# A two-layer graph attention network on one core: more sorted blocks, merged query products, a third fill bank, and exponentials kept beside the messages

## The chip, the core and the metric

The kernel runs on one core of a Trainium2 chip. The metric is the time of one execution on the device in microseconds; lower is better. The core has five engines that run their own instruction streams and meet at semaphores: PE (matrix products), DVE (vector work), ACT (activations and copies), POOL (here: indirect DMAs) and SP (plain DMAs).

## The reference

6250 nodes with 128 features and 200,000 edges, sorted by destination, with random sources. Each node also has an edge to itself. Two layers, 8 heads of 16:

```
loops = arange(n); src = [src, loops]; dst = [dst, loops]
for l in range(2):
    xn  = layernorm(x) * ln1_g + ln1_b
    deg = out-degree of each node, standardised
    xp  = xn + xn @ Wpos + bpos + deg * Wdeg + bdeg
    q, k, v = xp @ Wq + bq, xp @ Wk + bk, xp @ Wv + bv        # [n, 8, 16]
    att = clip(sum(q[dst] * k[src], -1) / 4, -50, 50)
    ex  = exp(att - segment_max(att, dst))
    aggr = segment_sum(v[src] * ex / segment_sum(ex, dst)[dst], dst)
    x = x + aggr @ Wo + bo
    x = x + gelu(layernorm(x) @ W1 + b1) @ W2 + b2
out = layernorm(input x + x)
```

## The kernel before

**Tables.** For each layer a table of keys and values (kv_table, 1 KB a node) and one of queries (q_table) lie in HBM. A prelude of about 280 us computes the first ones, the degrees and plans of the edges. The last steps of each node of layer 1 write its rows of layer 2's tables, and layer 2 starts when all are written.

**Two kinds of units.** The 49 tiles of 128 destination nodes are worked off in two ways.
- Most go by *chunks* of 1024 edges (8 tiles of 128 edges). `gather` (L1971, POOL) fetches the key and value rows of a chunk with 8 indirect DMAs, whose indices lie in SBUF (src_idx); four chunk buffers (kv_ring, and kv_last in the arena) take turns, and a buffer is free when the chunk's messages are made.
- The last NBS[l] tiles (8 in layer 1, 10 in layer 2) are *sorted blocks*: the edges of a tile are sorted by their source's tile during the run (`sort_vector`, `sort_tensor`), at most 128 to each pair of tiles. A tile is then 7 blocks (OB) of 7 edge tiles (TB). Their source rows come by one plain DMA into source_rows and are spread to the edges on PE by products with one-hot matrices (`source_by_edge` L940, `gather_rows` L952), and copied to kv_block by ACT (`copy_rows` L1238).

Layer 1 has 165 chunks and 56 blocks, layer 2 157 and 70. `unit_order` spreads the blocks among the chunks from chunk FIRST_B on.

**One unit.** PE computes distances between an edge's place and each node into one of two PSUM banks (*fills*, `fill_bank`; L962 "turn", L970 "hot"), ACT turns them into one-hots (L1227). PE spreads queries to the edges (L993 for a chunk, L1026 for a block) into two PSUM banks, DVE multiplies them by the keys in two operations (L1676), reduces to scores (L1685), clips (L1688, L1691); ACT takes the exponential twice, into PSUM (ex, L1260) and beside the messages in SBUF (msg, L1263); DVE multiplies the values by ex (L1700, the messages); PE sums them by destination (L1009, L1042), and DVE adds the sum to a ring of windows of 64 nodes (L1726) or to the block's row (L1731).

**The order** is written out: each engine's stream is a loop over slots, two a unit. In slot 2u PE makes the fills for unit u+2 and spreads unit u+1, DVE makes scores of u and products of u+1, ACT the exponentials of u; in slot 2u+1 DVE makes the messages of u and adds the sums of u-1, PE sums u-1. The 33 (27) steps of finished nodes and the steps of the sorts hang on the slots behind that. `exact_scale` (L1377) is the last part of a layernorm's scale, one short chain of three DVE steps, 196 times; L1896 and L1901 add degree and bias to a node's new q, k, v.

Of the kernel before, what the change touches and what calls it, by code (L numbers as in the profile page):

```python
# [68 lines left out]
OUT_TILES = 6  # L69
NEWTON = 3  # L70
# [5 lines left out]
NBS = 8, 10  # L76
# [13 lines left out]
RING_W = 32  # L90
AHEAD = 8
# [15 lines left out]
class Layer:  # L107


    def __init__(self, l, before):  # L110
# [10 lines left out]
        assert all(b - a > 2 for a, b in zip(self.block_at, self.block_at[1:]))  # L121
# [169 lines left out]
def graph_transformer(nc, x, src, dst, Wq, bq, Wk, bk, Wv, bv, Wo, bo, Wpos, bpos, Wdeg, bdeg,  # L291
                      ln1_g, ln1_b, ln2_g, ln2_b, W1, b1, W2, b2, out):
    with ExitStack() as ctx:
# [49 lines left out]
        small = sb("small", [P, 1])  # L343
# [24 lines left out]
        kv_block = part_of(TB * 2 * D).rearrange("p (t d) -> p t d", t=TB)  # L368
# [90 lines left out]
        tile_firsts = early[0:NS, free + 2 * SEG + 3 * P:free + 2 * SEG + 3 * P + SEG // P]  # L459
        block_firsts, tiles_before = (early[0:NS, o:o + NB] for o in range(free + 2 * SEG + 3 * P + SEG // P, free + 2 * SEG + 3 * P + SEG // P + 2 * NB, NB))  # L460
        o_less = free + 2 * SEG + 3 * P + SEG // P + 2 * NB
# [10 lines left out]
        ex = psum[:, 3, 0:T * H].rearrange("p (t h) -> p t h", t=T)  # L472
        apart = [psum[:, 4 + i, :] for i in range(2)]
# [16 lines left out]
        def edge_sum(l, u):  # L490
# [56 lines left out]
        next_ready, deg_row, qkv_ready, x_added = (  # L547
            semaphore(n) for n in ("next_ready", "deg_row", "qkv_ready", "x_added"))
# [11 lines left out]
        def bank_free(e, m, held):  # L560
# [4 lines left out]
            if before >= 0:  # L565
# [3 lines left out]
                elif name == "totals":  # L569
                    e.wait_ge(sort_total, (SA + 1) * j + 1)  # L570
                elif name.startswith("slots"):
                    e.wait_ge(sort_read, (SA + 3) * j + int(name[5:]) + 1)
                elif name.startswith("rank"):
                    e.wait_ge(sort_picked, 3 * (SA * j + int(name[4:])) + 1)
                else:
                    e.wait_ge(bank_read[name], nth(l, j, name))
# [348 lines left out]
        def fill_bank(e, k):  # L925
            if k >= 2:
                e.wait_ge(apart_read, k - 1)
            return apart[k % 2]

        def one_hots_made(e, k, since):  # L930

            if since < k + 2:
# [141 lines left out]
        def node_tensor(e, l, j, k, held):  # L1074
# [147 lines left out]
        def one_hots(e, to, n, what, h):  # L1222
# [4 lines left out]
            e.activation(to[:, at:at + width], apart[k % 2][:, 0:width], ACT.Relu, bias=1.0, scale=-1.0  # L1227
                         ).then_inc(apart_read, 1)

        def copy_rows(e, n, i):  # L1230

            m = part_of_unit(n)
            if m >= 1 and i == 0:
                e.wait_ge(msg_ready, block_unit(m - 1) + 1)
# [3 lines left out]
            e.copy(kv_block[:, ts[0]:ts[-1] + 1, :].rearrange("p t d -> p (t d)"), apart[k % 2][:, 0:len(ts) * 2 * D]  # L1238
# [15 lines left out]
        def make_exp(e, l, u):  # L1254
# [28 lines left out]
        def node_scale(e, l, j, i):  # L1283
# [4 lines left out]
            e.activation(tiny[:, 8:9], tiny[:, 7:8], ACT.Ln, bias=small[:, 0:1]).then_inc(norm_log, 1)  # L1288
            e.wait_ge(norm_log, n)
# [370 lines left out]
        def make_products(e, l, u):  # L1660
            n = unit(l, u)
            what, i = LAYERS[l].units[u]
            for h in range(2):
                f = 2 * n + h
                ts = part_tiles(l, u, h)
                rows = slice(ts[0], ts[-1] + 1)
                e.wait_ge(spread, f + 1)
                if what == "chunk":
                    m = chunk(l, i)
                    if h == 0:  # L1670
                        e.wait_ge(gathered[m % RING_KV], 16 * T * (m // RING_KV + 1))
                    keys = kv[m % RING_KV][:, rows, 0:D]
                else:
                    e.wait_ge(apart_read, fill(n, "rows", 2 * h + 1) + 1)
                    keys = kv_block[:, rows, 0:D]
                e.tensor_tensor(prod[:, ts[0] * P:(ts[-1] + 1) * P].rearrange("p (t d) -> p t d", d=D),  # L1676
# [510 lines left out]
```

## Time and profile before

| | us |
|---|---|
| median of 3 runs (3645.29 to 3647.68) | 3647.36 |
| span of the profiled execution | 5559.9 |
| busy in it: PE / DVE / POOL / ACT | 3461.6 / 2916.7 / 2472.4 / 1771.1 |

The page tells the share of each engine, the granted clock of TensorE by slices, the chain that ended last and the costliest groups. A group's row is: line, engine, operation, out<-in with shapes, count | busy us in all, mean ns of one | idle time of the engine just before them, and what ended most of it. "issue" is idle time for which the profile shows no reason, "remote" a wait whose cause it doesn't show. A row of the timeline is: start, duration, engine, line and operation, in brackets the idle time before. The profiled execution is much longer than a timed one.

### The profile page before, as it was taken

What the parts mean: (1) busy time and instruction counts of PE and PEld (TensorE: products, weight loads), DVE (VectorE), ACT (ScalarE), POOL (GpSimd) and SP (SyncE); (2) the same over time, 40 slices, a digit from 0 to 9 for tenths busy, and PEclk for the clock granted to TensorE, in tenths of its full rate; (3) what the DMA queues carried; (4) which work ended last, traced back from release to release, by engine and by line L of the source; (5) the groups of instructions that cost most, each with busy time, mean ns of one, the idle gap of its engine ahead of it and who ended that gap; (6) DMA issues with size and microseconds to landing.
All of it is one profiled execution on the core that took longest, in us unless ns stands there. A gap on an engine that the chain in (4) does not pass through costs nothing.

```text
span 5559.9 us, 72300 instructions
## 1 busy us (share of the span) xinstructions
PE 3461.6 (62%) x24196; PEld 2666.6 (48%) x24475; DVE 2916.7 (52%) x6780; ACT 1771.1 (32%) x4391; POOL 2472.4 (44%) x2597
## 2 busy tenths in 40 slices
PE   5834656655665656666566376666666566666666
PEld 4623445444454445444444254455555455545545
DVE  9944545554454545555455354554554454545455
ACT  2301232323333332323234133333333333333334
POOL 1065444444444444444542544445444454444443
PEclk7756777777777777777777677777777777777777
DMA  2133333333333333333332333333333333333332
GB/s 73 49 111 87 88 106 93 102 88 95 102 94 99 94 102 89 104 95 96 107 105 65 106 103 109 108 107 113 96 108 106 108 110 113 111 102 115 109 104 73
DMA packets 404556, 548.28 MB, mean 99 GB/s; under 512 B 78348, under 2 KB 318656, under 8 KB 403988
## 3 DMA queue, kind: packets, MB, share of 16 engines
q0 software_dynamic: 123648, 337.81, 20.9%
q1 hardware_dynamic: 273030, 198.56, 11.9%
q10 hardware_dynamic: 7506, 7.20, 0.4%
q8 instruction: 203, 3.33, 0.2%
q14 instruction: 169, 1.38, 0.1%
HBM read 518.00 MB, written 25.29 MB: 98 GB/s over the span
## 4 chain that ended last, share of the span: by engine, by line
PE 32%; another core or an unknown queue 30%; DVE 14%; issue 12%; ACT 10%; DVEq 0%; SPq 0%; DMA 0%; ACTq 0%
PE psum L952 7%; PE psum L993 4%; PE psum L1009 3%; ACT scratch L1227 3%; PE psum L1042 3%; PE psum L1026 3%; DVE att L1685 2%; PE psum L970 2%; ACT arena L1238 2%; DVE scratch L1676 2%; DVE kv_ring L1394 1%; PE psum L1123 1%; DVE work L1377 1%; DVE scratch L1700 1%
## 5 line engine op out<-in xcount | busy, mean ns | idle before, releaser
L1971 POOL DMA_INDIRECT kv_ring<-kv_table,src_idx x1936 | 1846.4, 954 | 2132.8 <-DVE scratch L1700 1501.1
L1227 ACT ACTIVATE scratch<-psum 128x512 f32<-128x512 f32 x1148 | 649.5, 570 | 2061.3 <-remote 1442.0
L952 PE MATMUL psum<-arena 128*128 128x256 f32 x1764 | 631.5, 486 | 464.2 <-issue 194.2
L1971 POOL DMA_INDIRECT arena<-kv_table,src_idx x640 | 607.8, 950 | 664.6 <-DVE scratch L1700 489.7
L1726 DVE SCALAR_TENSOR_TENSOR arena<-psum,in_block,arena 128x136 f32 x644 | 200.9, 353 | 1286.4 <-remote 1187.3
L993 PE MATMUL psum<-q_win,scratch 64*128 64x128 f32 x5152 | 534.3, 349 | 285.7 <-issue 149.9
L952 PEld LDWEIGHTS psum<-arena 128*128 128x128 f32 x1764 | 372.6, 236 | 621.0 <-issue 319.2
L1009 PE MATMUL psum<-scratch 128*64 128x136 f32 x5152 | 519.1, 330 | 185.4 <-issue 154.2
L993 PEld LDWEIGHTS psum<-q_win,scratch 64*128 64x128 f32 x5152 | 443.2, 243 | 343.1 <-issue 332.5
L1238 ACT COPY arena<-psum 128x512 f32<-128x512 f32 x504 | 265.1, 532 | 986.9 <-remote 524.7
L1685 DVE TENSOR_REDUCE att<-scratch 128x64 f32<-128x1024 f32 (+1 forms) x448 | 525.1, 1172 | 0.1
L1676 DVE TENSOR_TENSOR scratch<-psum,arena 128x512 f32<-128x512 f32 (+1 forms) x412 | 255.4, 646 | 507.4 <-remote 397.5
L1009 PEld LDWEIGHTS psum<-scratch 128*64 128x64 f32 x5152 | 376.8, 161 | 268.6 <-issue 245.6
L1676 DVE TENSOR_TENSOR scratch<-psum,kv_ring 128x512 f32<-128x512 f32 x484 | 313.7, 684 | 264.5 <-remote 182.6
L1026 PE MATMUL psum<-q_win,scratch 128*128 128x128 f32 x1764 | 272.1, 318 | 288.4 <-ACT arena L1238 270.5
L1042 PE MATMUL psum<-scratch 128*128 128x136 f32 x1764 | 309.2, 332 | 3.8 <-ACT work L1326 3.8
L1700 DVE TENSOR_TENSOR scratch<-kv_ring,psum 128x1024 f32<-128x1024 f32 x242 | 292.3, 1208 | 29.4 <-ACT psum L1260 24.2
L1042 PEld LDWEIGHTS psum<-scratch 128*128 128x128 f32 x1764 | 289.6, 238 | 8.6 <-issue 4.5
L1026 PEld LDWEIGHTS psum<-q_win,scratch 128*128 128x128 f32 x1764 | 273.4, 234 | 12.7 <-issue 3.9
L962 PEld LDWEIGHTS psum<-plan_mem,places 128*128 128x128 bf16 x322 | 35.9, 112 | 423.5 <-issue 372.6
L1700 DVE TENSOR_TENSOR scratch<-arena,psum 128x896 f32<-128x896 f32 (+1 forms) x206 | 232.1, 1127 | 9.0 <-ACT psum L1260 7.4
L1731 DVE TENSOR_TENSOR arena<-arena,psum 128x136 f32<-128x136 f32 x108 | 31.9, 295 | 330.6 <-PE psum L1042 200.0
(251 smaller groups left out, 4873.9 us busy)
## 6 DMA issues: line engine op xcount, KB each, us to landing
arena<-kv_table SPq DMA_DIRECT2D x126, 896.0 KB
kv_ring<-kv_table,src_idx POOLq DMA_INDIRECT x1936
q_win<-q_table SPq DMA_DIRECT2D x644, 32.0 KB
work<-kv_table SPq DMA_DIRECT2D x98, 128.0 KB
arena<-kv_table,src_idx POOLq DMA_INDIRECT x640
q_win<-q_table SPq DMA_DIRECT2D x126, 64.0 KB
work<-q_table SPq DMA_DIRECT2D x98, 64.0 KB
kv_table<-work SPq DMA_DIRECT2D x49, 128.0 KB
```

The source lines that it names most:

```text
L952: mm = e.matmul(to[:, t % 2 * 2 * D:(t % 2 + 1) * 2 * D], hot_source[:, t * P:(t + 1) * P], source_rows[:, t, :], start=True, stop=True)
L993: m = e.matmul(q_edge[h][:, t * P:(t + 1) * P], hotT[n % 2][h * HALF:(h + 1) * HALF, t * P:(t + 1) * P], q_win[h * HALF:(h + 1) * HALF, n ...
L1009: m = e.matmul(to[h * HALF:(h + 1) * HALF], by_edge[:, t * P + h * HALF:t * P + (h + 1) * HALF], msg[n % 2][:, h * T // 2 + t, :], start=t ...
L1026: m = e.matmul(q_edge[f % 2][:, (t - ts[0]) * P:(t - ts[0] + 1) * P], hotT[n % 2][:, t * P:(t + 1) * P], q_win[:, n % 2, :], start=True, s ...
L1042: m = e.matmul(edge_sum(l, u), hot[n % 2][:, t, :], msg[n % 2][:, t, :], start=t == 0, stop=t == last)
L1227: e.activation(to[:, at:at + width], apart[k % 2][:, 0:width], ACT.Relu, bias=1.0, scale=-1.0).then_inc(apart_read, 1)
L1238: e.copy(kv_block[:, ts[0]:ts[-1] + 1, :].rearrange("p t d -> p (t d)"), apart[k % 2][:, 0:len(ts) * 2 * D]).then_inc(apart_read, 1)
L1676: e.tensor_tensor(prod[:, ts[0] * P:(ts[-1] + 1) * P].rearrange("p (t d) -> p t d", d=D), q_edge[f % 2][:, 0:len(ts) * P].rearrange("p (t ...
L1685: e.tensor_reduce(raw_att.rearrange("p t h -> p (t h)"), prod[:, 0:ts * P].rearrange("p (g d) -> p g d", d=HD), AX_X, ALU.add).then_inc(sc ...
L1700: e.tensor_tensor(msg[n % 2][:, 0:ts, 0:D].rearrange("p t (h d) -> p t h d", d=HD), values.rearrange("p t (h d) -> p t h d", d=HD), ex[:, ...
L1726: e.scalar_tensor_tensor(out=row, in0=of_edges, scalar=in_block[:, k, i:i + 1], in1=row, op0=ALU.mult, op1=ALU.add).then_inc(acc_added, 1)
L1971: e.indirect_dma_start(kv[m % RING_KV][:, t, :], None, kv_table[l], bass.IndirectOffsetOnAxis(ap=src_idx[:, c * T + t:c * T + t + 1], axis ...
```

## The change

- NBS 8, 10 becomes 10, 12: two tiles of each layer go from chunks to blocks. Layer 1 has 157 chunks and 70 blocks, layer 2 149 and 84. The prelude counts the edges of 12 tiles instead of 10 (13 counting steps instead of 11), and 12 sorts are done instead of 10. Blocks may now stand two units apart.
- `make_products` is one operation over both PSUM banks. It waits for both halves of the spread.
- ACT takes the exponential once, into msg; the messages read it there. Bank 3 of PSUM, where ex lay, is the third fill bank.
- kv_block is double. The ring of windows has 16 rows instead of 32, which makes the space.
- Smaller ones: the sort's reduction writes bf16 itself (L1772, L1774 before); `exact_scale` has two DVE steps, with a short ACT operation beside (L1288 before); b_next enters qkv through a product with a row of ones on PE, and degree and sum are one DVE operation (L1896, L1901 before).

```diff
+FILL_BANKS = 3
-NBS = 8, 10
+NBS = 10, 12
-RING_W = 32
-AHEAD = 8
+RING_W = 16
+AHEAD = 4
...
-        kv_block = part_of(TB * 2 * D).rearrange("p (t d) -> p t d", t=TB)
+        kv_blocks = [part_of(TB * 2 * D).rearrange("p (t d) -> p t d", t=TB) for _ in range(2)]
...
         q_edge = [psum[:, i, :] for i in range(2)]
-        ex = psum[:, 3, 0:T * H].rearrange("p (t h) -> p t h", t=T)
-        apart = [psum[:, 4 + i, :] for i in range(2)]
+        q_edges = psum[:, 0:2, :].rearrange("p b n -> p (b n)")
+        apart = [psum[:, 3 + i, :] for i in range(FILL_BANKS)]
...
         def fill_bank(e, k):
-            if k >= 2:
-                e.wait_ge(apart_read, k - 1)
-            return apart[k % 2]
+            if k >= FILL_BANKS:
+                e.wait_ge(apart_read, k + 1 - FILL_BANKS)
+            return apart[k % FILL_BANKS]
...
             elif name == "qkv":
                 e.wait_ge(next_ready, i + 1)
-                e.matmul(ps[:, 0:QKV], col, w_qkv[:, l + 1, :], start=True, stop=True).then_inc(done, 1)
+                e.matmul(ps[:, 0:QKV], ones[0:1, :], b_next[0:1, :], start=True, stop=False)
+                e.matmul(ps[:, 0:QKV], col, w_qkv[:, l + 1, :], start=False, stop=True).then_inc(done, 1)
...
         def copy_rows(e, n, i):
-            if m >= 1 and i == 0:
-                e.wait_ge(msg_ready, block_unit(m - 1) + 1)
+            if m >= 2 and i == 0:
+                e.wait_ge(msg_ready, block_unit(m - 2) + 1)
...
         def make_exp(e, l, u):
             e.wait_ge(score_ready, n + 1)
-            e.activation(ex[:, 0:ts], att[:, n % 2, 0:ts], ACT.Exp).then_inc(exp_ready, 1)
             if n >= 2 and u + 2 >= LAYERS[l].nu:
                 e.wait_ge(edge_summed, n - 1)
-            e.activation(msg[n % 2][:, 0:ts, D:MW], att[:, n % 2, 0:ts], ACT.Exp)
+            e.activation(msg[n % 2][:, 0:ts, D:MW], att[:, n % 2, 0:ts], ACT.Exp).then_inc(exp_ready, 1)
...
         def make_products(e, l, u):
...
-            for h in range(2):
-                f = 2 * n + h
-                e.wait_ge(spread, f + 1)
...
-                e.tensor_tensor(prod[:, ts[0] * P:(ts[-1] + 1) * P].rearrange("p (t d) -> p t d", d=D),
-                                q_edge[f % 2][:, 0:len(ts) * P].rearrange("p (t d) -> p t d", d=D), keys, ALU.mult
-                                ).then_inc(prod_ready, 1)
...
+            e.wait_ge(spread, 2 * n + 2)
+            e.tensor_tensor(prod[:, 0:ts * P].rearrange("p (t d) -> p t d", d=D),
+                            q_edges[:, 0:ts * P].rearrange("p (t d) -> p t d", d=D), keys, ALU.mult
+                            ).then_inc(prod_ready, 2)
...
         def make_messages(e, l, u):
             e.wait_ge(exp_ready, n + 1)
             e.tensor_tensor(msg[n % 2][:, 0:ts, 0:D].rearrange("p t (h d) -> p t h d", d=HD),
                             values.rearrange("p t (h d) -> p t h d", d=HD),
-                            ex[:, 0:ts].unsqueeze(3).to_broadcast([P, ts, H, HD]), ALU.mult).then_inc(msg_ready, 1)
+                            msg[n % 2][:, 0:ts, D:MW].unsqueeze(3).to_broadcast([P, ts, H, HD]), ALU.mult
+                            ).then_inc(msg_ready, 1)
...
         def exact_scale(e, l, j, i):
-            step(e.scalar_tensor_tensor, out=t, in0=v, scalar=EPS, in1=y, op0=ALU.add, op1=ALU.mult)
-            step(e.scalar_tensor_tensor, out=t, in0=t, scalar=-0.5, in1=y, op0=ALU.mult, op1=ALU.mult)
+            step(e.scalar_tensor_tensor, out=t, in0=y, scalar=minus_half, in1=y, op0=ALU.mult, op1=ALU.mult)
             step(e.scalar_tensor_tensor, out=y, in0=t, scalar=1.5, in1=y, op0=ALU.add, op1=ALU.mult)
...
-            elif k == 29:
-                e.scalar_tensor_tensor(out=qkv, in0=wz_next[:], scalar=deg_z[:, j:j + 1], in1=b_next[:], op0=ALU.mult,
-                                       op1=ALU.add).then_inc(deg_row, 1)
             elif k == 31:
-                e.tensor_tensor(qkv, ps("qkv")[:, 0:QKV], qkv, ALU.add).then_inc(qkv_ready, 1)
+                e.scalar_tensor_tensor(out=qkv, in0=wz_next[:], scalar=deg_z[:, j:j + 1], in1=ps("qkv")[:, 0:QKV],
+                                       op0=ALU.mult, op1=ALU.add).then_inc(qkv_ready, 1)
```

DVE, in layer 1, a chunk unit whose messages come after the products of the block behind it (with a node's or a sort's steps between them); before:

```order
L1685 TENSOR_REDUCE att<-scratch 128x64
L1688 TENSOR_SCALAR att_clip<-att 128x64
L1691 SCALAR_TENSOR_TENSOR att<-att,att_clip 128x64
L1676 TENSOR_TENSOR scratch<-psum,arena 128x512
L1676 TENSOR_TENSOR scratch<-psum,arena 128x384
L1896 SCALAR_TENSOR_TENSOR work<-wz_next,deg_z,b_next 128x384
L1883 TENSOR_TENSOR x_all<-x_all,psum 128x128
L1830 BN_STATS work<-x_all 128x6
L1832 BN_AGGR work<-work 128x2
L1700 TENSOR_TENSOR scratch<-arena,psum 128x8x128
```

Now (scores L1683 to L1689, products L1674, node steps L1378 and L1890, sort L1777 and L1780, messages L1698):

```order
L1683 TENSOR_REDUCE att<-scratch 128x64
L1686 TENSOR_SCALAR att_clip<-att 128x64
L1689 SCALAR_TENSOR_TENSOR att<-att,att_clip 128x64
L1674 TENSOR_TENSOR scratch<-psum,arena 128x896
L1378 SCALAR_TENSOR_TENSOR work<-work 128x1 x2
L1890 TENSOR_SCALAR work<-x_all,work 128x128
L1777 TENSOR_TENSOR arena<-arena,iota_rep 128x1280
L1780 TENSOR_TENSOR arena<-arena 128x490 x2
L1698 TENSOR_TENSOR scratch<-kv_ring,scratch 128x8x128
```

The products are one row of 896 (1024 for a chunk) instead of two, and the messages read scratch (msg) in place of psum (ex).

PE, early in layer 2, from the spread of a block's queries on (L1026; L1070, L1071 and L1063 are a sort's, L1109, L1110, L1113 and L1117 a node's); before:

```order
L1026 MATMUL psum<-q_win,scratch 128x128 x7
L1117 MATMUL psum<-work,w 128x128 x4
L1070 MATMUL psum<-arena,before 128x490
L1071 MATMUL psum<-arena,ones_b 128x490
L970 MATMUL psum<-places,plan_mem 128x128 x4
L1009 MATMUL psum<-scratch 64x136 x8
L1063 MATMUL psum<-arena 98x128 x10
L962 MATMUL psum<-plan_mem,places 128x512
L993 MATMUL psum<-q_win,scratch 128x128 x8
L940 MATMUL psum<-arena,places 128x512
L940 MATMUL psum<-arena,places 128x384
```

Now:

```order
L1026 MATMUL psum<-q_win,scratch 128x128 x4
L940 MATMUL psum<-arena,places 128x512
L1026 MATMUL psum<-q_win,scratch 128x128 x3
L940 MATMUL psum<-arena,places 128x384
L1063 MATMUL psum<-arena 98x128 x10
L970 MATMUL psum<-places,plan_mem 128x128 x4
L1009 MATMUL psum<-scratch 64x136 x8
L1113 MATMUL psum<-ident,work 128x128
L962 MATMUL psum<-arena,places 128x512
L993 MATMUL psum<-q_win,scratch 128x128 x8
L952 MATMUL psum<-arena 128x256 x2
```

The source fills of the next block (L940) stood one chunk after the spread; now they stand between its two halves, and that block's rows (L952) are gathered in the very next chunk's slot.

## Rows read from the trace of the kernel before

**Rows 1.** The page's first line, and TensorE's granted clock in 40 slices (tenths).
```profile
span 5559.9 us, 72300 instructions
...
PEclk7756777777777777777777677777777777777777
```

**Rows 2.** Timeline of POOL: first gathers, first of layer 2, last gather.
```profile
278.64 9.23 POOL L1971 DMA_INDIRECT kv_ring<-kv_table,src_idx  x1 [27.59 <-DMA kv_table<-scratch]
288.18 0.95 POOL L1971 DMA_INDIRECT kv_ring<-kv_table,src_idx  x1 [0.30 <-issue]
...
3053.18 0.94 POOL L1971 DMA_INDIRECT kv_ring<-kv_table,src_idx  x1 [70.25 <-DMA kv_table<-work]
...
5501.81 0.95 POOL L1971 DMA_INDIRECT kv_ring<-kv_table,src_idx  x1 [0.30 <-issue]
```

**Rows 3.** The page's groups of instructions: the gathers.
```profile
L1971 POOL DMA_INDIRECT kv_ring<-kv_table,src_idx x1936 | 1846.4, 954 | 2132.8 <-DVE scratch L1700 1501.1
...
L1971 POOL DMA_INDIRECT arena<-kv_table,src_idx x640 | 607.8, 950 | 664.6 <-DVE scratch L1700 489.7
```

**Rows 4.** Timeline of DVE and POOL at four places where both are at work.
```profile
347.40 1.17 DVE L1759 TENSOR_TENSOR arena<-arena,iota_rep 128x1960 bf16<-128x1960 bf16 x1
347.58 1.80 POOL L1971 DMA_INDIRECT kv_ring<-kv_table,src_idx  x1 [0.30 <-issue]
...
646.87 0.61 DVE L1896 SCALAR_TENSOR_TENSOR work<-wz_next,deg_z,b_next 128x384 f32<-128x384 f32 x1
647.03 1.26 POOL L1971 DMA_INDIRECT kv_ring<-kv_table,src_idx  x1 [0.30 <-issue]
...
2702.79 1.08 DVE L1700 TENSOR_TENSOR scratch<-arena,psum 128x896 f32<-128x896 f32 x1
2702.96 0.95 POOL L1971 DMA_INDIRECT kv_ring<-kv_table,src_idx  x1 [0.30 <-issue]
...
2825.74 0.61 DVE L1896 SCALAR_TENSOR_TENSOR work<-wz_next,deg_z,b_next 128x384 f32<-128x384 f32 x1
2825.74 0.95 POOL L1971 DMA_INDIRECT kv_ring<-kv_table,src_idx  x1 [0.30 <-issue]
```

**Rows 5.** Groups of instructions of DVE, each shape apart.
```profile
L1676 DVE TENSOR_TENSOR scratch<-psum,kv_ring 128x512 f32<-128x512 f32 x484 | 313.7, 684 | 264.5 <-remote 182.6 <-issue 45.4 <-PE psum L993 35.9
L1700 DVE TENSOR_TENSOR scratch<-kv_ring,psum 128x1024 f32<-128x1024 f32 x242 | 292.3, 1208 | 29.4 <-ACT psum L1260 24.2 <-issue 5.3
...
L1700 DVE TENSOR_TENSOR scratch<-arena,psum 128x896 f32<-128x896 f32 x126 | 135.3, 1074 | 2.7 <-ACT psum L1260 1.6 <-issue 0.9
...
L1779 DVE TENSOR_TENSOR arena<-arena,iota_rep 128x1280 bf16<-128x1280 bf16 x40 | 32.7, 818 | 0.0
...
L1896 DVE SCALAR_TENSOR_TENSOR work<-wz_next,deg_z,b_next 128x384 f32<-128x384 f32 x49 | 29.7, 607 | 0.0
...
L1759 DVE TENSOR_TENSOR arena<-arena,iota_rep 128x1960 bf16<-128x1960 bf16 x10 | 11.7, 1170 | 0.0
```

**Rows 6.** Timeline of PE at the upper clock: parts of a block and a chunk.
```profile
2736.91 1.72 PE L1026 MATMUL psum<-q_win,scratch 128*128 128x128 f32 x14 [1.66 <-issue]
2739.24 0.40 PE L970 MATMUL psum<-places,plan_mem 128*128 128x128 bf16 x4 [0.61 <-ACT arena L1238]
2739.57 1.15 PE L1009 MATMUL psum<-scratch 128*64 128x136 f32 x16
2740.64 0.39 PE L962 MATMUL psum<-plan_mem,places 128*128 128x512 bf16 x1
2741.05 1.16 PE L993 MATMUL psum<-q_win,scratch 64*128 64x128 f32 x16
...
2761.14 1.13 PE L952 MATMUL psum<-arena 128*128 128x256 f32 x4
```

**Rows 7.** Timeline of PE where it waits for nothing that the profile shows.
```profile
1995.82 0.37 PE L993 MATMUL psum<-q_win,scratch 64*128 64x128 f32 x1 [1.73 <-issue]
1997.97 0.37 PE L1117 MATMUL psum<-work,w 128*128 128x128 f32 x1 [1.79 <-issue]
```

More of the change, by code:

```diff
@@ L120, in __init__ @@
         self.block_at = [u for u, (what, _) in enumerate(self.units) if what == "block"]
-        assert all(b - a > 2 for a, b in zip(self.block_at, self.block_at[1:]))
+        assert all(b - a > 1 for a, b in zip(self.block_at, self.block_at[1:]))
         self.tiles = sorted(range(NT), key=lambda j: (self.last_unit(j), j))
@@ L1226, in one_hots @@
             e.wait_ge(apart_made, k + 1)
-            e.activation(to[:, at:at + width], apart[k % 2][:, 0:width], ACT.Relu, bias=1.0, scale=-1.0
+            e.activation(to[:, at:at + width], apart[k % FILL_BANKS][:, 0:width], ACT.Relu, bias=1.0, scale=-1.0
                          ).then_inc(apart_read, 1)
@@ L1237, in copy_rows @@
             e.wait_ge(apart_made, k + 1)
-            e.copy(kv_block[:, ts[0]:ts[-1] + 1, :].rearrange("p t d -> p (t d)"), apart[k % 2][:, 0:len(ts) * 2 * D]
+            e.copy(kv_blocks[m % 2][:, ts[0]:ts[-1] + 1, :].rearrange("p t d -> p (t d)"), apart[k % FILL_BANKS][:, 0:len(ts) * 2 * D]
                    ).then_inc(apart_read, 1)
@@ L1288, in node_scale @@
             e.activation(tiny[:, 8:9], tiny[:, 7:8], ACT.Ln, bias=small[:, 0:1]).then_inc(norm_log, 1)
+            e.activation(tiny[:, 10:11], tiny[:, 7:8], ACT.Identity, scale=-0.5, bias=small[:, 1:2])
             e.wait_ge(norm_log, n)
@@ L1662, in make_products @@
             what, i = LAYERS[l].units[u]
[L1663 to L1678 removed]
+            ts = LAYERS[l].tiles_of(u)
+            if what == "chunk":
+                m = chunk(l, i)
+                e.wait_ge(gathered[m % RING_KV], 16 * T * (m // RING_KV + 1))
+                keys = kv[m % RING_KV][:, 0:ts, 0:D]
+            else:
+                m = part_number(l, i)
+                e.wait_ge(apart_read, fill(n, "rows", 3) + 1)
+                keys = kv_blocks[m % 2][:, 0:ts, 0:D]
+            e.wait_ge(spread, 2 * n + 2)
+            e.tensor_tensor(prod[:, 0:ts * P].rearrange("p (t d) -> p t d", d=D),
+                            q_edges[:, 0:ts * P].rearrange("p (t d) -> p t d", d=D), keys, ALU.mult
+                            ).then_inc(prod_ready, 2)
         def make_scores(e, l, u):
@@ L1697, in make_messages @@
             ts = LAYERS[l].tiles_of(u)
-            values = kv[chunk(l, i) % RING_KV][:, :, D:2 * D] if what == "chunk" else kv_block[:, :, D:2 * D]
+            values = (kv[chunk(l, i) % RING_KV] if what == "chunk" else kv_blocks[part_number(l, i) % 2])[:, :, D:2 * D]
             e.wait_ge(exp_ready, n + 1)
@@ L1769, in sort_vector @@
                 elif k == 8 + 3 * q and q < SA:
-                    whole = by_run(s_lo.bitcast(F32))[:, q]
-                    e.wait_ge(sort_picked, 3 * (SA * s + q) + 1)
-                    e.tensor_reduce(whole, s_sel.rearrange("p b g -> p g b"), AX_X, ALU.add).then_inc(sort_picked, 1)
-                    e.wait_ge(sort_picked, 3 * (SA * s + q) + 2)
-                    e.tensor_copy(by_run(s_rank)[:, q], whole).then_inc(sort_picked, 1)
+                    e.wait_ge(sort_picked, 2 * (SA * s + q) + 1)
+                    with nc.allow_low_precision(reason="one of the terms is a whole number up to 128, the others are 0"):
+                        e.tensor_reduce(by_run(s_rank)[:, q], s_sel.rearrange("p b g -> p g b"), AX_X, ALU.add
+                                        ).then_inc(sort_picked, 1)
                 elif k == 9 + 3 * q and q < SA:
-                    e.wait_ge(sort_picked, 3 * (SA * s + q) + 3)
+                    e.wait_ge(sort_picked, 2 * (SA * s + q) + 2)
                     if SA * s + q:
```

21 lines of the change are left out of this document (10 added, 11 removed).

## The prediction

> **What bounds the kernel now.** I read four views: the page's head and its row of the granted clock, the gathers on POOL in order of time, the groups of instructions, and short stretches of the timeline in which DVE and POOL run side by side. The first thing to see is that the profiled execution took 5559.9 us and the timed ones 3647 us, so a third of the profiled span isn't there in a timed run. Where it goes can be seen on PE: in a row of products that wait for nothing, one matmul starts 2.15 us after the other [rows 1, 7]. So shares of the profiled span say little, and "POOL is idle for 2133 us before its gathers, mostly for DVE's messages" [rows 3] says only that POOL, like the rest, waits for a PE that trickles.
>
> What POOL costs when nobody holds it up does carry over. Each edge tile of a chunk is one indirect DMA; it starts 1.25 us after the one before (0.95 busy, 0.30 idle), all through the trace [rows 2]. There are 322 chunks of 8, so 2576 of them [rows 3]. The time of a kernel whose POOL never waits inside a layer: 278.6 us to the first gather, 9.5 for that one, 1319 more in layer 1 at 1.25 = 1649, 70 between the layers (layer 2 reads the table that the last node of layer 1 writes), 1256 at 1.25 = 1570, and 57 from the last gather's end to the end of the span [rows 1, 2]. Sum: 3634 us. The timed median is 3647. A sum with no wait in it that lands 13 us below the measurement is my reason to take POOL's gathers as the bound of both layers: DVE, PE and ACT then have slack, and chunks are four buffers deep, so that slack absorbs their unevenness.
>
> **What holds a gather up.** A gather is longer than 0.95 us in a few places, and each time the same thing stands beside it. The one at 347.58 took 1.80: DVE's op of L1759, with both inputs in SBUF, ran from 347.40 to 348.57. The one at 647.03 took 1.26: L1896, again two inputs in SBUF, ran until 647.48 [rows 4]. Both fit one law: the gather reads its indices 0.13 us after its start, and if such an op holds DVE then, it waits until the op's end (348.57 - 347.71 = 0.86 of wait for 0.85 seen; 647.48 - 647.16 = 0.32 for 0.31). An op begun only 0.13 us before the read does not hold it: at 2825.74 the gather took 0.95 with L1896 beside it. An op with one input in PSUM never does: L1700 begun at 2702.79, 0.30 us before the read, left the gather at 0.95 [rows 4]. Gathers come every 1.25 us, so an op of length L meets (L - 0.145)/1.25 reads and delays by half of L - 0.145 on average: (L - 0.145)^2 / 2.5. Today's ops of this kind cost L1779 40 x 0.18 = 7.2, L1759 10 x 0.42 = 4.2, L1896 49 x 0.085 = 4.2 us [rows 5], which puts the sum at 3650.
>
> The Trainium skill ("SBUF — State Buffer", the section on two separate sides) says the same of the ports: VectorE and GpSimd share one pair, which a DVE op with two SBUF inputs locks for its whole length against a GpSimd op that reads SBUF, and whoever starts first gets it. The trace agrees on the wait (0.85 and 0.31 us above), less on its extent: to the letter the lock is the whole op, which would make 306 x 0.584 + 154 x 0.461 = 250 us of the messages below and 3738 of the sum, where the gather at 2825.74 decides for the shorter hold. The rule speaks against this change.
>
> **Part by part.**
> Fewer gathers: 306 chunks instead of 322, 128 gathers less at 1.25 us = **-160 us** on the path.
>
> The messages: they read the exponentials from msg (SBUF) where they read them from ex (PSUM), so L1700's op gets two inputs in SBUF. Its length stays: 1.208 us for 1024 elements, 1.074 for 896 [rows 5]. By the law 306 x 1.063^2 / 2.5 = 306 x 0.452 = 138 and 154 x 0.929^2 / 2.5 = 154 x 0.345 = 53: **+191 us**. This assumes that messages fall anywhere between two gathers; the bounds are 0 (they always miss) and 306 x 1.06 + 154 x 0.93 = 468 (they always hit at their start). I take the mean: DVE's node and sort work is unevenly spread ahead of each message, as between 647 and 649 us.
>
> Other two-input ops: two sorts more, 2 x (0.42 + 4 x 0.18) = +2.3; the addition of L1896 is gone, and its successor reads PSUM, -4.2. The prelude counts 13 steps of 32 tiles instead of 11: by L1779's 0.82 us for 1280 elements a step costs DVE about 1.5 us, so +3.
>
> Products in one operation: 1024 elements in one op should take what L1700 takes, 1.21 against 2 x 0.684 [rows 5], 0.16 us less of DVE a unit. A block's first product no longer starts beside the spread of its second half, 0.5 us of latency. Both lie under the gathers: nothing on the path; if DVE bound, -74 us (460 x 0.16).
>
> PE: 28 blocks more, 16 chunks less. At the upper clock a chunk takes 0.33 + 1.07 + 0.41 + 1.16 = 3.0 us (L970, L1009, L962 from start to start, L993) and a block 3.5 x 1.13 (L952) + 1.72 (L1026) + 1.8 (L1042, alike) + 0.7 + 4 fills of 0.4 = 9.8 [rows 6]. That is 28 x 9.8 - 16 x 3.0 = **+226 us of PE work**, plus some 30 for the bias rows of qkv and 20 for two sorts; hidden while the gathers bind, with the cover given below. In layer 2 some blocks now have a single chunk between them.
>
> Third fill bank: PE may write a fill while ACT still reads the two before. It changes no order, only how far PE can run ahead; nothing on a path that POOL sets. One exponential less per unit and a few more block fills on ACT cancel nearly; ACT is the idlest engine. A second kv_block lets the rows of a block be copied before the block ahead has its messages: needed for the closer blocks, no gain by itself. The ring of 16 must be cleared earlier: chunk i needs tile (i/2 - 11)/2, whose last edges came 18 chunks ago; no wait. The shorter scale chain, the sort's direct write and the qkv addition shorten DVE by less than 100 us in all, hidden.
>
> **Sum** against the median, since the skeleton above is worth as much: 3647.4 - 160 + 191 + 2.3 - 4.2 + 3 = **3680 us**, 0.9% slower.
>
> **Rivals.**
> A (the sum), 3680. For it: both laws come from this trace. Against: that the pace of 1.25 us holds in a timed run rests on one coincidence of sums.
> B, the messages don't hold the gathers. The op isn't in the trace in its new form, and messages could fall into a fixed place between gathers. Then 3647 - 160 + 3 = 3490. Against it: all of L1759, L1779, L1896 obey the law, in bf16 and f32.
> C, PE becomes the bound. It has 226 + 50 us more to do, while the sum gives it 33 us more time. With no slack today that is 3647 + 276 = 3923; it decides once today's slack is under 243 us. The row of the granted clock shows 0.7 to 0.8 in most slices [rows 1], and each stretch at the lower level doubles these prices; but a timed run has fewer stalls and so, I think, less of it. I put the slack at about 150: 3775.
> D, the gathers aren't the bound today: unprofiled they come faster than every 1.25 us, and PE, ACT and DVE bind by waiting for one another. Then the messages' holds are hidden, fewer DVE operations (74 for the products, 49 x 0.61 = 30 for L1896) and the third bank shorten that loop, and PE's extra work lengthens it, partly overlapped. About -50: 3600. The sum of 3634 speaks against it.
>
> **How the numbers follow.** A 0.48, C 0.18, B 0.14, D 0.20. A measurement of this kernel can tell 0.2% (7 us) from no change. Faster: B, and D but for its upper end, 0.30. The same: edges of D and A, 0.07. Slower: 0.63. The range 3570 to 3790 holds A, nearly all of D and most of C, and leaves out B and a PE without slack.
>
> **What would show it.** In the profile after: messages with two SBUF inputs beside gathers of more than 0.95 us, so a mean duration of the gather group near 954 + 191/2448 us = 1.03 us where POOL is running as densely as in a timed run, and less in the profile by POOL's idle share, some 0.98 to 1.0; starts still 0.30 us behind the last end. If the mean stays at 0.95, B. If the gathers wait for the messages as before and the time rises beyond 3740, C. The products should read 1.2 us. The forecast is wrong at its root if a kernel with the messages' exponentials back in PSUM isn't faster than the changed one.

## The result and the profile after

The changed kernel takes **3808.4 us** (median of 4 runs, 3798.2 to 3825.6) where the kernel before took 3646.3 beside it. The ratio of the two is put at 1.0453, 95% interval 1.0422 to 1.0483. The forecast was 3680, with 3570 to 3790 around it: the sign is right, the size is outside the range.

The profiled execution of before that [rows 1 to 7] come from was stretched to 5559.9 us. What stretched it isn't shown. A second one of the same kernel wasn't stretched, so the comparison is made against that one. Its page, the first line, the busy times and the gathers:

```profile
span 3641.7 us, 72300 instructions
...
PE 2880.4 (79%) x24196; PEld 2279.3 (63%) x24475; DVE 2892.9 (79%) x6780; ACT 1760.8 (48%) x4391; POOL 2480.0 (68%) x2597
...
L1971 POOL DMA_INDIRECT kv_ring<-kv_table,src_idx x1936 | 1849.1, 955 | 690.7 <-issue 584.3
...
L1971 POOL DMA_INDIRECT arena<-kv_table,src_idx x640 | 612.7, 957 | 196.6 <-issue 192.8
```

The changed kernel, the same lines and the granted clock (tenths, 40 slices), which answer [rows 1, 3]:

```profile
span 3812.6 us, 74017 instructions
...
PE 3120.4 (82%) x25398; PEld 2506.9 (66%) x25705; DVE 2896.4 (76%) x6187; ACT 1821.4 (48%) x4404; POOL 2513.6 (66%) x2470
...
PEclk6785789899898989989999799889998989999997
...
L1965 POOL DMA_INDIRECT kv_ring<-kv_table,src_idx x1840 | 1878.1, 1021 | 732.9 <-issue 543.8
...
L1965 POOL DMA_INDIRECT arena<-kv_table,src_idx x608 | 617.2, 1015 | 273.5 <-issue 179.8
```

TensorE's mean granted clock was 0.889 in the second trace of before and 0.888 here, so the clock as a whole isn't what changed the time. There are 128 gathers fewer, each some 63 ns longer, and POOL's idle time before them is 119 us more. What that idle time is stands in the list of POOL's waits (who waits <- for whom: us in all, times, longest), first of before, then of after:

```profile
POOL kv_ring L1971 <- DVE scratch L1700: 21.8, 17, 3.9
POOL arena L1971 <- DVE scratch L1700: 3.7, 7, 1.3
```
```profile
POOL kv_ring L1965 <- DVE scratch L1698: 109.3, 55, 9.3
POOL arena L1965 <- DVE scratch L1698: 93.7, 18, 9.5
```

The chain that ended last tells it by engine. Before:

```profile
POOL 39%; PE 20%; DVE 18%; issue 15%; ACT 5%; DMA 2%; DVEq 0%; another core or an unknown queue 0%; SPq 0%; POOLq 0%; ACTq 0%
```

After:

```profile
PE 44%; DVE 25%; issue 8%; ACT 7%; POOL 6%; DMA 5%; SPq 2%; DVEq 1%; another core or an unknown queue 0%; POOLq 0%; ACTq 0%
```

The chain left POOL. For the second trace of before I had set a sign ahead: waits for messages under 30 us in all mean that the gathers bind, 100 us or more that they don't. It has 18. So the span can be taken apart along POOL's stream (the 0.30 us that lies between any two gathers is taken off each wait; "over 0.945" is what the gathers behind the first took beyond that length each; in brackets the number of waits):

| us | before | after | difference |
|---|---|---|---|
| first gather begins | 283.9 | 285.5 | +1.6 |
| 128 gathers of 1.25 | | | -160.0 |
| gathers over 0.945 | 25.6 | 177.3 | +151.7 |
| waits for messages inside layers | 18.3 (11) | 180.2 (68) | +161.9 |
| gap between the layers | 49.1 | 46.7 | -2.4 |
| last gather's end to the end | 44.2 | 58.5 | +14.3 |
| sum | | | +167 |

The spans differ by 171; of the rest, 2.5 us are the first gather, which took 7.04 us instead of 4.54. Three terms have some 150 to 160 us each: the gain of the fewer gathers, the holds by the messages, and waits that the forecast had at zero.

### The profile page after: what moved, and what is told of

It reads as the page before. It is cut to its first block, busy times and chain, and to the rows that moved or that the text cites. A ratio compares the mean times of both kernels' runs of the same rounds, so it can differ in the third digit from the quotient of the medians.

```text
span 3812.6 us, 74017 instructions
## 1 busy us (share of the span) xinstructions
PE 3120.4 (82%) x25398; PEld 2506.9 (66%) x25705; DVE 2896.4 (76%) x6187; ACT 1821.4 (48%) x4404; POOL 2513.6 (66%) x2470
## 3 DMA queue, kind: packets, MB, share of 16 engines
q14 instruction: 162, 1.33, 0.1%
## 4 chain that ended last, share of the span: by engine, by line
PE 44%; DVE 25%; issue 8%; ACT 7%; POOL 6%; DMA 5%; SPq 2%; DVEq 1%; another core or an unknown queue 0%; POOLq 0%; ACTq 0%
PE psum L952 12%; PE psum L1042 6%; POOL kv_ring L1965 5%; PE psum L993 4%; PE psum L1026 4%; DVE att L1683 4%; PE psum L1063 2%; DVE scratch L1674 2%; PE psum L1009 2%; DVE work L1378 2%; DVE kv_ring L1395 2%; DMA q_win<-q_table 2%; PE psum L1123 2%; PE psum L970 2%; DVE scratch L1698 2%
## 5 line engine op out<-in xcount | busy, mean ns | idle before, releaser
L1228 ACT ACTIVATE scratch<-psum 128x512 f32<-128x512 f32 (+1 forms) x1228 | 679.5, 568 | 553.0 <-PE psum L970 201.0
L952 PE MATMUL psum<-arena 128*128 128x256 f32 x2156 | 673.1, 435 | 73.1 <-ACT scratch L1228 43.9
L1239 ACT COPY arena<-psum 128x512 f32<-128x512 f32 x616 | 327.3, 532 | 580.5 <-PE psum L952 577.9
L993 PE MATMUL psum<-q_win,scratch 64*128 64x128 f32 x4896 | 410.0, 314 | 169.1 <-DVE scratch L1674 80.4
L952 PEld LDWEIGHTS psum<-arena 128*128 128x128 f32 x2156 | 422.9, 216 | 177.1 <-ACT scratch L1228 58.3
L1683 DVE TENSOR_REDUCE att<-scratch 128x64 f32<-128x1024 f32 (+1 forms) x460 | 536.0, 1165 | 0.1
L993 PEld LDWEIGHTS psum<-q_win,scratch 64*128 64x128 f32 x4896 | 346.8, 214 | 263.7 <-issue 166.5
L1009 PE MATMUL psum<-scratch 128*64 128x136 f32 x4896 | 373.2, 297 | 17.4 <-ACT work L1322 6.3
L1674 DVE TENSOR_TENSOR scratch<-psum,kv_ring 128x1024 f32<-128x1024 f32 x230 | 280.3, 1219 | 139.6 <-DMA kv_ring<-kv_table,src_idx 92.4
L1674 DVE TENSOR_TENSOR scratch<-psum,arena 128x896 f32<-128x896 f32 (+1 forms) x230 | 260.2, 1131 | 131.7 <-PE psum L1026 89.0
L1009 PEld LDWEIGHTS psum<-scratch 128*64 128x64 f32 x4896 | 292.2, 143 | 52.5 <-issue 21.5
L1263 ACT ACTIVATE scratch<-att 128x64 f32<-128x64 f32 (+1 forms) x460 | 116.9, 254 | 428.1 <-DVE att L1689 426.5
L1698 DVE TENSOR_TENSOR scratch<-arena,scratch 128x896 f32<-128x896 f32 (+1 forms) x230 | 259.0, 1126 | 59.0 <-ACT scratch L1263 58.9
L1698 DVE TENSOR_TENSOR scratch<-kv_ring,scratch 128x1024 f32<-128x1024 f32 x230 | 279.2, 1214 | 27.0 <-ACT scratch L1263 26.5
L1026 PE MATMUL psum<-q_win,scratch 128*128 128x128 f32 x2156 | 275.0, 278 | 17.4 <-DVE scratch L1674 7.2
L1026 PEld LDWEIGHTS psum<-q_win,scratch 128*128 128x128 f32 x2156 | 274.5, 195 | 21.9 <-issue 11.7
```

The costliest lines, as they stand in the source:

```text
L952: mm = e.matmul(to[:, t % 2 * 2 * D:(t % 2 + 1) * 2 * D], hot_source[:, t * P:(t + 1) * P], source_rows[:, t, :], start=True, stop=True)
L993: m = e.matmul(q_edge[h][:, t * P:(t + 1) * P], hotT[n % 2][h * HALF:(h + 1) * HALF, t * P:(t + 1) * P], q_win[h * HALF:(h + 1) * HALF, n ...
L1009: m = e.matmul(to[h * HALF:(h + 1) * HALF], by_edge[:, t * P + h * HALF:t * P + (h + 1) * HALF], msg[n % 2][:, h * T // 2 + t, :], start=t ...
L1026: m = e.matmul(q_edge[f % 2][:, (t - ts[0]) * P:(t - ts[0] + 1) * P], hotT[n % 2][:, t * P:(t + 1) * P], q_win[:, n % 2, :], start=True, s ...
L1228: e.activation(to[:, at:at + width], apart[k % FILL_BANKS][:, 0:width], ACT.Relu, bias=1.0, scale=-1.0).then_inc(apart_read, 1)
L1239: e.copy(kv_blocks[m % 2][:, ts[0]:ts[-1] + 1, :].rearrange("p t d -> p (t d)"), apart[k % FILL_BANKS][:, 0:len(ts) * 2 * D]).then_inc(apa ...
```

## Experiments

All ratios are against the kernel before on the same chip. Its median beside the experiments was 3648.8 to 3651.1, against 3646.3 beside the 3808.4, so a difference between times of two experiments is uncertain by some 5 us. "Waits" and "over 0.945" are worked out as above.

**1. The exponentials beside the messages, alone.** The kernel before with one part of the change:

```diff
-            e.activation(ex[:, 0:ts], att[:, n % 2, 0:ts], ACT.Exp).then_inc(exp_ready, 1)
...
-            e.activation(msg[n % 2][:, 0:ts, D:MW], att[:, n % 2, 0:ts], ACT.Exp)
+            e.activation(msg[n % 2][:, 0:ts, D:MW], att[:, n % 2, 0:ts], ACT.Exp).then_inc(exp_ready, 1)
...
-                            ex[:, 0:ts].unsqueeze(3).to_broadcast([P, ts, H, HD]), ALU.mult).then_inc(msg_ready, 1)
+                            msg[n % 2][:, 0:ts, D:MW].unsqueeze(3).to_broadcast([P, ts, H, HD]), ALU.mult).then_inc(msg_ready, 1)
```

> One part of the change alone, in the kernel before: the exponential is taken once, into msg, and the messages read it there (two SBUF inputs); banks, blocks and products as before. Theory H: the holds are fully on the path, 322 x 0.452 + 126 x 0.345 = 189 us less what clumps, 3790 to 3840. Theory P (gathers have slack): under 40 us, 3640 to 3690.

Measured: 3814.2 us, ratio 1.0461 (1.0437 to 1.0484). POOL's gathers and its waits for messages in it:

```profile
POOL kv_ring L1970 <- DVE scratch L1699: 0.9, 3, 0.3
...
L1970 POOL DMA_INDIRECT kv_ring<-kv_table,src_idx x1936 | 1983.3, 1024 | 661.3 <-issue 588.2
```

POOL hardly ever waits, its gathers are 175 us longer in all, the 18 us of waits are gone, and the time is some 165 us more (the spans of the two traces differ by 158). So the gathers bound the kernel before, and the holds are real: where gathers bind, a microsecond of hold is a microsecond of time.

**2. The changed kernel with 8 and 10 blocks.**

```diff
-NBS = 10, 12
+NBS = 8, 10
```

> The changed kernel with the blocks as they were, 8 and 10; the rest of the change stays. Theory H: 128 gathers come back (+160) and the holds stay at 189, so 3800 to 3850, no faster than the changed kernel. Theory P: PE loses 226 us of work, the time falls back to 3640 to 3700.

Measured: 3815.6 us, ratio 1.046 (1.0435 to 1.0486); waits 0.0, gathers over 0.945 210.1 us. The 128 gathers more cost nothing that shows: with 10 and 12 blocks their 160 us come back as 180 us of waits.

**3. The exponentials back in PSUM, in the changed kernel.** They need their bank, so the third fill bank goes with them.

```diff
-FILL_BANKS = 3
+FILL_BANKS = 2
...
-        apart = [psum[:, 3 + i, :] for i in range(FILL_BANKS)]
+        ex = psum[:, 3, 0:T * H].rearrange("p (t h) -> p t h", t=T)
+        apart = [psum[:, 4 + i, :] for i in range(FILL_BANKS)]
...
-                            msg[n % 2][:, 0:ts, D:MW].unsqueeze(3).to_broadcast([P, ts, H, HD]), ALU.mult
-                            ).then_inc(msg_ready, 1)
+                            ex[:, 0:ts].unsqueeze(3).to_broadcast([P, ts, H, HD]), ALU.mult).then_inc(msg_ready, 1)
```

> The changed kernel with that part undone: two exponentials, one into PSUM bank 3 for the messages, and so two fill banks again; 10 and 12 blocks and one product stay. Theory H: the 177 us by which its gathers are longer than 0.945 go, 3600 to 3660. Theory P: the added PE work of the blocks binds, and two banks instead of three cost a little more: 3770 to 3850.

Measured: 3962.7 us, ratio 1.0848 (1.0811 to 1.0885). POOL's waits and gathers:

```profile
POOL kv_ring L1966 <- DVE scratch L1700: 325.3, 133, 9.5
...
POOL arena L1966 <- DVE scratch L1700: 197.7, 37, 11.9
...
L1966 POOL DMA_INDIRECT kv_ring<-kv_table,src_idx x1840 | 1757.4, 955 | 939.5 <-issue 520.5
```

The holds are gone (955 ns), and the time rises by 154 us, beyond both of the ranges that I had set: waits of 469 us take their place. More than one thing was changed at once here, so the next run takes the bank by itself.

**4. The third fill bank.** The changed kernel with two banks for the fills, all else as it is.

```diff
-FILL_BANKS = 3
+FILL_BANKS = 2
...
-        apart = [psum[:, 3 + i, :] for i in range(FILL_BANKS)]
+        apart = [psum[:, 4 + i, :] for i in range(FILL_BANKS)]
```

> The changed kernel with two fill banks instead of three; the exponentials stay in SBUF. The version with the exponentials in PSUM and two banks took 3963 with 469 us of POOL's waits. If the third bank is what kept the changed kernel from that (theory B3): 3930 to 4050. If the third bank is worth nothing, as forecast: 3800 to 3830, and the 155 us between those two come from the place of the exponentials.

Measured: 3944.7 us, ratio 1.0799 (1.077 to 1.0828): the third bank is worth 136 us in the changed kernel. PE's waits for ACT to have read a fill bank (L1228 makes one-hots of it, L1239 copies a block's rows out of it), the longest with two banks:

```profile
PE psum L952 <- ACT arena L1239: 76.8, 150, 0.8
PE psum L970 <- ACT arena L1228: 76.2, 98, 1.7
...
PE psum L962 <- ACT scratch L1228: 63.5, 79, 1.7
```

and with three:

```profile
PE psum L962 <- ACT arena L1228: 55.3, 40, 1.9
PE psum L952 <- ACT scratch L1228: 43.9, 50, 2.0
```

All waits of PE for L1228 and L1239 together are 239 us with two banks and 109 with three, those for L1239 being gone: 130 us, near the 136.

Beside experiment 3 it says something more: with two banks the kernel without holds (3963) isn't faster than the one with them (3945). So the holds cost little there. That they cost nothing isn't shown, since the kernel without holds also takes a second exponential on ACT in every unit (ACT is busy for 1905.8 us against 1840.5).

**5. The loop without the gathers.** Three kernels in which every second gather of a chunk is left out once the four buffers have been filled, so POOL binds nothing; the keys and values of half the chunks' edges are stale, all other work is done.

```diff
-                        e.wait_ge(gathered[m % RING_KV], 16 * T * (m // RING_KV + 1))
+                        e.wait_ge(gathered[m % RING_KV], 8 * T * (m // RING_KV + 2))
...
-            for t in range(T):
+            for t in range(0, T, 1 if m < RING_KV else 2):
```

> The kernel before with every second gather of a chunk left out (after the first four chunks), so that half of the edge tiles of a chunk carry old rows: it leaves out work, and its time is that of PE, DVE and ACT without a bound by POOL. Theory H (gathers bind before: POOL waited 18 us in all in its trace): well below 3646, 3300 to 3550. Theory P: 3600 or more.

> The changed kernel with every second gather of a chunk left out (after the first four chunks), which leaves out work in the same way. Theory H+P (the loop of PE, ACT and DVE has become as long as the gathers: POOL waited 180 us in its trace): little below 3808, 3650 to 3760, and above the same edit of the kernel before by 150 or more. Theory H alone (only the holds count): as far below as the kernel before falls, 3400 to 3550.

> The changed kernel (three banks, exponentials beside the messages, products in one operation) with 8 and 10 sorted blocks, and with every second gather of a chunk left out once the buffers have been filled: so the keys and values of half the edges of the chunks are stale, all else is computed. With the gathers at half their number nothing on POOL binds, and the time is that of the loop of PE, ACT and DVE. The same cut gave 3722 with 10 and 12 blocks and 3494 in the kernel before. Theory that the 28 further blocks lengthen the loop: by PE's work (226 + 20 + 20 us of the forecast) the loop falls to 3400 to 3480. Rival, the blocks cost the loop little, and something else in the change (the wait of the one product for both halves, or the exponentials that the messages now wait for) does: 3600 to 3720.

| every second gather left out | median | ratio (95%) | granted clock | PE busy | span less PE busy |
|---|---|---|---|---|---|
| kernel before, 8 and 10 blocks | 3493.7 | 0.9579 (0.9554 to 0.9603) | 0.909 | 2870.2 | 616 |
| changed kernel, 8 and 10 blocks | 3422.3 | 0.937 (0.9338 to 0.9403) | 0.895 | 2856.8, with missing records some 2890 | 569, or some 536 |
| changed kernel, 10 and 12 blocks | 3722.3 | 1.0201 (1.0158 to 1.0244) | 0.893 | 3143.8 | 584 |

The busy lines of the last two:

```profile
PE 2856.8 (83%) x24302; PEld 2288.0 (67%) x24583; DVE 2810.6 (82%) x6047; ACT 1697.8 (50%) x4145; POOL 1313.8 (38%) x1326
```
```profile
PE 3143.8 (84%) x25705; PEld 2487.7 (67%) x25705; DVE 2884.2 (77%) x6187; ACT 1821.6 (49%) x4404; POOL 1239.5 (33%) x1262
```

The first of these traces isn't complete: it has 24302 of PE's products for 24583 weight loads (the PEld count), while the other two kernels of the table have one for each. The 281 that it lacks are all products of 512 columns that make a fill. Put in behind their weight loads with 0.4 us each, they cover some 33 us in which PE seems idle; that gives the second figures in the table, which are an estimate. The traces of before and after lack as many (24196 of 24475 and 25398 of 25705), so their busy times can be compared as they stand.

This settles the main question. The loop had 3646 - 3494 = 152 us of slack before (with a granted clock of 0.909 where the full kernel had 0.889, so some of the 152 may be clock). Apart from the blocks, the change makes it 72 us shorter. The 28 blocks (with 16 chunks fewer and two sorts more) make it 300 us longer, of which some 250 are PE's busy time and some 50 are time in which PE waits. So PE's added work goes into the loop whole, and the loop alone, with half of the gathers out of its way, needs 3722 us: 229 more than before, against 152 of slack.

**6. The products in two operations again.**

```diff
-            e.wait_ge(spread, 2 * n + 2)
...
+            for h in range(2):
+                ts = part_tiles(l, u, h)
+                if what == "block":
+                    e.wait_ge(apart_read, fill(n, "rows", 2 * h + 1) + 1)
+                e.wait_ge(spread, 2 * n + h + 1)
```

> The changed kernel with the products in two operations again, each after its half of the spread. If the merged product costs latency (a block's first product no longer runs beside the spread of its second half, theory L): 3700 to 3790, POOL's waits fall by half. If it only saves DVE 0.13 us a unit: 3808 to 3860.

Measured: 3778.6 us, ratio 1.0367 (1.0335 to 1.0399), so one operation costs 30 us (POOL's waits fell from 180 to 111 us, not quite by half). The products of a block (line, shapes, count | busy, mean ns | idle before, by whom), merged and then split:

```profile
L1674 DVE TENSOR_TENSOR scratch<-psum,arena 128x896 f32<-128x896 f32 x154 | 167.5, 1087 | 90.1 <-PE psum L1026 89.0 <-issue 0.6
```
```profile
L1676 DVE TENSOR_TENSOR scratch<-psum,arena 128x512 f32<-128x512 f32 x306 | 202.9, 684 | 87.6 <-PE psum L1026 46.0 <-DMA arena<-kv_table,src_idx 25.9 <-PE psum L993 15.0
```

The merged one saves 0.15 us a block and 0.14 a chunk of DVE's work, and waits 43 us more for a block's spread (89.0 against 46.0).

**7. The smaller edits, and one block tile more.** The kernel before with the double kv_block, the ring of 16, the two-step scale, the bias through PE and the sort's direct write; products, exponentials and fill banks as before. Then 8 and 11, or 9 and 10 block tiles. Of the edit against the changed kernel only the line of the blocks is shown; the rest puts back what experiments 3 and 6 put back:

```diff
-NBS = 10, 12
+NBS = 8, 10
```

> The kernel before with the change's smaller edits alone: double kv_block, ring of 16 windows, two-step scale, bias through PE, direct write of the sort; 8 and 10 blocks, products in two operations, exponentials in PSUM, two fill banks. Theory (gathers bind, 1.25 us each, no holds by messages): 3646 less the 4 us of L1896's holds, 3635 to 3648, the gathers wait less than 25 us in all. Rival, the smaller edits are part of the loss (a slower loop on PE by the bias products and on ACT by the scale step): above 3660 with more waits of POOL.

> As small_edits_8_10, but with one sorted block tile more in layer 2 (8 and 11): 5 chunks or some 32 to 40 gathers fewer, 7 blocks more. If the loop of PE, ACT and DVE has slack under the gathers (152 us in the kernel before, by its version with half of them) and a tile of blocks costs the loop some 57 to 60 us while it takes 40 to 50 off the gathers, layer 2 stays bound by the gathers: 3600 to 3620, which would beat both kernels. Rival, slack is local (chunks beside a block are late at once, as in after_ex_psum, where 28 blocks gave 469 us of waits): 3640 to 3680.

> As small_edits_8_10, but with one sorted block tile more in layer 1 (9 and 10). 3600 to 3620 if the slack of layer 1 covers 7 blocks; layer 1 has the heavier node steps beside its chunks (32 of them, with the tables of layer 2), and in the changed kernel 128 of the 180 us of waits lay there, so I expect it 10 to 30 us behind small_edits_8_11. Rival: above 3660.

| | median | ratio (95%) | waits in layer 1 / 2 |
|---|---|---|---|
| 8 and 10 | 3661.3 | 1.0027 (1.001 to 1.0044) | 37.6 / 0.0 |
| 8 and 11 | 3694.6 | 1.0127 (1.0094 to 1.016) | 29.9 / 65.6 |
| 9 and 10 | 3703.3 | 1.015 (1.0119 to 1.0181) | 108.1 / 1.0 |

All three miss the times that I expected; 8 and 10 and 9 and 10 fall where their rivals had them (above 3660), 8 and 11 lies above its rival's range too (3640 to 3680). The smaller edits cost some 10 us instead of saving 4. One tile more takes 40 us off the gathers and returns 58 us (8 and 11) or 72 us (9 and 10) of waits, all in the layer it was added to. No kernel of this study that does all the work is faster than the one before.

## Why the forecast missed

**The skeleton held.** "Gathers every 1.25 us bind both layers" was read from a trace stretched by half, and from a sum that came within 13 us. The unstretched trace has the same pace (0.95 + 0.30 us) and 18 us of waits. That the sum came so near was in part luck: with the unstretched trace's start, first gather, gap between the layers and end (283.9, 4.8, 49 and 44 us instead of 278.6, 9.5, 70 and 57) it makes 3600, and the waits and the longer gathers fill the rest. Experiment 1 shows the bound itself, and rival D's 3600 is out: with the gathers halved the kernel before ran in 0.958 of its time.

**The law of the holds held; its even spread didn't quite.** For the 448 messages of experiment 1 it gives 322 x 0.452 + 126 x 0.345 = 189 us; the gathers grew by 175. In the changed kernel it gave 191, and they grew by 152.

Counted gather by gather in the traces, the law itself is right. In experiment 1, 348 gathers had their read due inside a message (from 0.145 us behind its start to its end); the law, applied to each, gives 169 us and they took 169 more. They end 0.82 us behind the message's end. In the changed kernel it is 303 gathers, 149 us by the law and 147 measured. What was too high is the assumption that messages fall anywhere between two gathers: it makes 367 and 375 such gathers. Why fewer are met isn't shown. That POOL stands idle for 162 us more can be part of it, but with two banks it stood idle for 307 us and 292 were met, held for 150 us in all.

The rule of the Trainium skill ("SBUF — State Buffer", two separate sides), taken to the letter as a lock for the op's whole length, made 250. The traces agree with the wait and not with that extent: in experiment 1 the 63 gathers whose read was due within the first 0.15 us of a message have a median of 0.95 us. Rival B is out. The markers came as written: a mean gather of 1.02 us, products of 1.22; so did the sign for C (waits for the messages, and a time beyond 3740).

But the law missed one thing: operations with two inputs in SBUF that follow one another without a gap hold on together. In the changed kernel's timeline (start, duration, engine, line) L1799 held the gather, and L1698, begun after the gather's read of its indices was due, held it on:

```profile
1327.28 0.65 DVE L1799 TENSOR_TENSOR arena<-earlier,arena 40x490 bf16<-40x490 bf16 x1
...
1327.61 2.28 POOL L1965 DMA_INDIRECT arena<-kv_table,src_idx  x1 [0.30 <-issue]
1327.86 1.21 DVE L1698 TENSOR_TENSOR scratch<-kv_ring,scratch 128x1024 f32<-128x1024 f32 x1
```

The gather ended at 1329.89, 0.82 us after L1698; it took 0.82 us from its read on elsewhere too (0.95 less 0.13). Few gathers are of this kind, so it weighs little in the sum.

**What failed is the cover of PE's work.** The forecast priced that work well: 226 + 50 us in all, and PE's busy time rose by 240 (2880.4 to 3120.4) at the same granted clock; 226 + 20 for the blocks and two sorts, against some 250 in experiment 5. It then put it at nothing, "hidden while the gathers bind". But a gain of 160 us on the gathers takes away the cover under which it would be hidden, and the loop's 229 us more were never covered by 152 of slack. I had the slack right in rival C (150; measured 152), and the condition as well ("it decides once today's slack is under 243 us"); 152 is under 243. So by my own numbers C was met, and I gave it 0.18 against 0.48 for A. The error was to hold the slack for the doubtful number and the sum for the safe one, and to count the holds as 33 us more time for PE. C's mechanism isn't the whole of it either: its 3775 is nearer, but the loop alone takes 3722, and the last 86 us stand in no rival.

**The third bank, too, was put at nothing.** "Nothing on a path that POOL sets" is true of the kernel before; in the changed one, where PE sets the path, it is worth 136 us. Without it the time is 3945. For the same reason the merged products aren't free (30 us): the wait of 0.5 us that I named for a block's product lies on the loop's path. So the bank's gain, which the forecast hadn't, made up for part of what it missed elsewhere. Experiment 7's smaller edits show it in small: PE's busy time rose from 2880 to 2926 us, nearly all of it the product that brings in the bias (47 us where I had 30), and 37.6 us of waits stand where 18.3 were. From the groups of small_edits_9_10:

```profile
L1131 PE MATMUL psum<-b_next,ones 1*128 1x384 f32 x98 | 47.2, 562 | 11.9 <-ACT work L1337 10.5 <-ACT work L1345 1.3
```

**The rest: two near bounds make more than the larger of the two.** The gathers alone need 3813 - 180 = 3633 us (holds included), the loop alone 3722, and the kernel takes 3808, 86 more than the larger. The waits show why. They aren't spread: the nine longest of 68 are 7.7 to 9.2 us each and make up 77 of the 180 us, and all nine lie where a tile is being sorted. These 12 stretches (from 10 us before a sort's first L1063 to 10 us behind its last) are some 820 us long and hold 115 of the 180 us. One such place, where a sort's product on PE (L1063) waits for the sort's step on DVE (L1791), with the spread of the next chunk (L993) queued behind it:

```profile
1338.55 2.63 PE L1063 MATMUL psum<-arena 128*98 128x128 bf16 x10 [1.84 <-DVE arena L1791]
...
1341.54 2.08 PE L993 MATMUL psum<-q_win,scratch 64*128 64x128 f32 x16
...
1343.79 1.23 DVE L1674 TENSOR_TENSOR scratch<-psum,kv_ring 128x1024 f32<-128x1024 f32 x1 [3.11 <-PE psum L993]
...
1346.49 1.22 DVE L1698 TENSOR_TENSOR scratch<-kv_ring,scratch 128x1024 f32<-128x1024 f32 x1 [0.34 <-ACT scratch L1263]
...
1347.98 0.94 POOL L1965 DMA_INDIRECT kv_ring<-kv_table,src_idx  x1 [5.47 <-DVE scratch L1698]
```

Here the gathers are ahead and stand still for 5.47 us. PE runs at the lower level of its clock in it (granted clock 0.5 from 1336.3 to 1346.5): L993 takes 2.08 us and four products of L952 take 2.07 just behind, against 1.16 and 1.13 at the upper level [rows 6]. The mean granted clock is 0.84 in the sorts' stretches and 0.92 in the rest behind the first gather. So the clock is part of such waits, but not of all: in the 15 us that end with the wait it was 1.0 at four of the nine longest. Between such places the loop waits for the gathers (L1674 waited 92.4 + 24.9 us for them in all). Four buffers, 40 us of gathers, don't carry one stretch's surplus to the next. Experiment 7 agrees in part: one tile more returned 58 and 72 us of waits for 40 us of gathers, and with 9 and 10 tiles 108 of 109 us of them lie in sorts' stretches; but with 8 and 11 only 53 of 96 do. So sorts are where most waits are, not the only cause of them. That the two bounds change places along the run is read from these waits; no run tests it. How much of the 86 us is due to the holds, and how much would stand with gathers that are never held, isn't settled: a kernel with three fill banks and the exponentials in PSUM needs a ninth bank, and wasn't run.

**The forecast's test of its root was badly put.** "The exponentials back in PSUM isn't faster than the changed one" came true (3963), and yet the holds are real. The test moved a PSUM bank along with the operand. Alone, in the kernel before, the step gives +165 us.

## What to carry to other kernels

When work goes from the engine that binds to one that has slack, compare the slack with the added work first, and against the bound after the gain: 152 us of slack can't hide a loop that grows by 229, however well the binding engine is understood. Measure the slack by leaving out part of the binding engine's work; it took one kernel here. And when two bounds lie near each other (here 3633 and 3722), allow for more than the larger one: here it was 86 us more, with four buffers between them.

## What the runs showed that was not expected

- A profiled execution can be stretched by half (5559.9 against 3641.7 us of the same kernel). The pace of the gathers (1.25 us) and the lengths of DVE's operations (1208 and 1206 ns for the messages of a chunk) were the same in both; PE's gaps and POOL's waits for messages weren't: 1991 us before ([rows 3], 1501.1 + 489.7) against 25.5.
- A gather is held through a chain of operations that touch, 1.33 us in one case, where each alone would have held it for 0.2 or not at all.
- A third PSUM bank for products that ACT reads gave 136 us of 3945 with no instruction changed; PE works in order, and with two banks each fill waits for the read of the one before the last.
